# A decoder layer on one core: first maxima in banks of four diagonal squares or of the squares below them, a third cross tile's scores copied out by ScalarE, and the steps in another order

## The chip, the cores and the metric

One NeuronCore of a Trainium2 chip runs the whole kernel. The metric is the device time of one execution in microseconds (us). TensorE (PE) multiplies matrices, VectorE (DVE), ScalarE (ACT) and GpSimd (POOL) do the elementwise work, and SyncE (SP) issues most DMAs. The kernel is written in an explicit form: each engine runs its own list of instructions in order, and semaphores are the only tie between the lists.

## The reference

```python
x = layernorm(x + self_attention(x))          # 4 x 512 tokens of 256, 16 heads of 16, causal
x = layernorm(x + cross_attention(x, ctx))    # 16 heads of 64, 64 context rows of 192 per batch
x = layernorm(x + experts(x))                 # 8 experts, 256 -> 1024 -> 256, top 2, exact gelu
```

The self attention is a softmax over scores / 4 with everything above the diagonal masked; q, k and v have biases. The cross attention is a softmax over 64 context rows. The expert part routes each token to the two experts with the largest logits, weighs their outputs with a softmax over the two, and adds them. All is float32 in and out; the kernel multiplies in float16 pairs of a high and a low part (the function `three` issues three matmuls for one product).

## The kernel before

The program has two blocks. `attention_block` computes both attentions of all four batches and ends with the logits of most tokens; `expert_block` routes, gathers tokens by indirect DMA, runs 23 tiles of one or two blocks of 128 slots through their experts, scatters, adds and normalizes. The change touches only the first block.

Inside `attention_block` all work is cut into steps written `kind:batch:index`, and one long text, `ORDER`, lists them. Every engine goes through the whole list in that order and runs its own part of each step, so `ORDER` fixes the order within each engine. PSUM is shared by two rings: three banks M (kinds `xT, mT, ct, cx, o, xa, O, rt, lg, m, S, T`) and two double banks R (kinds `s, q, v, cT, W, kv, A, VW, idle`). `Slots` gives the steps of a ring their banks in the order of `ORDER`; PE waits until the previous user of a bank has been read out. PV is one more bank for the weighted sums.

The steps of a batch, in the order in which they depend on one another:

- `xT`, `q`, `v`: transpose the tokens, project. `ql` (POOL) makes the low parts, `store` and `stack` (SP) write q and k to DRAM and read them back as stacks of 48 rows per head pair (`qs`, `ks`), 12 DMAs.
- `m` (22 steps, index into `MAXES`): first pass over the scores, only for the row maxima. A step fills two M banks, one for the even and one for the odd heads, adds the causal mask by a matmul with `causal` (L227), and DVE reduces each bank (L237) into `rowmax`. `va` (POOL) adds the bias to v.
- `mT`, `max`: transpose the maxima (L964), negate (ACT, L646), write them as one more row of `qs` by two small DMAs.
- `s` (20 steps): the scores again, shifted by the maxima (PE L974), exponential (ACT L655), mask on the diagonal squares (POOL L526). `w` (12): weighted sums into PV (L988), `pv` (ACT L659) copies them, `ct`, `ct.n` transpose and divide.
- `cx`, `o`, `o.d`, `r`, `n`: transpose, output projection, residual, layernorm (`r` is the root on POOL, `n` the scaling on DVE).
- `x1b`, `xa`: add the bias (POOL), transpose. `S` (8 steps, two for each of four token tiles): cross scores. They leave PSUM in one of two ways. `S.d` (DVE): maximum over each head (L800), then the difference is written to `e_x` (L801). Or, for the last tile only, `S.c` (ACT, L668) copies both halves, `S.m` (DVE, L808) takes the maxima from SBUF, and `S.p` (POOL, L556) subtracts them. Then `xe` (exponential, ACT), `xs` (sum, DVE), `xp` (division, POOL L561), `T`, `T.l` (transposes, L1030), `O`, `O.d` (weighted sum and projection in one, 24 matmuls, L210), `r`, `n` into `x2_all`.
- `rt`, `lg`: router transposes and logits for 12 of the 16 token tiles.

The steps `cT, wk, W, kv, wo, A, VW` with `A.s`, `VW.s` (SP) fold the cross attention's weights with the context once for all batches and store the result in DRAM; `ax` and `vw` load the part of a batch. `idle:k:n` issues n matmuls of 512 columns on PE whose result nobody reads (L885); there are 129 of them: 43 ahead of the first `m`, 42 in fourteen groups of three between the `m` steps of batch 0, 16 each ahead of the `m` steps of batches 2 and 3, and 12 in the last batch's tail.

The work is interleaved across batches. While batch b's self attention runs (`s`, `w`), the `m` steps of batch b+1 run, and batch b-1's cross attention. Only batch 0's `m` steps and batch 3's cross attention stand nearly alone.

## Time and profile before

| | us |
|---|---|
| median of 3 runs | 726.97 |
| lowest, highest | 723.96, 730.16 |
| the profiled execution, whole | 724.8 |
| its span from the first to the last instruction | 723.1 |
| busy in the span: PE, DVE | 609.1, 534.3 |
| busy in the span: ACT, POOL | 393.3, 327.5 |

An engine is busy in the profile when an instruction that does work is on it. Matmuls are pipelined, so PE's busy time is an upper bound of what it needs. Weight loads (PEld) run beside the matmuls. The granted TensorE clock is given as a share of full speed. The idle time ahead of a group is followed by the engine and line that ended it.

### The profile page before, as it was taken

Reading aid. Unit: us, or ns where it says so; the run is one execution under the profiler, and the core shown is the slowest. Engines: PE = TensorE matmul, PEld = TensorE weight load, DVE = VectorE, ACT = ScalarE, POOL = GpSimd, SP = SyncE. Lnnn points to the kernel's source line nnn. Section 1 sums busy time; section 2 is a strip of 40 time slices with the busy share of each in tenths; the row PEclk is TensorE's granted clock in tenths of the full one; section 3 lists DMA queues with packets and bytes.
Section 4 is the critical chain, followed back from the end, with each engine's and each line's share of the span. In section 5 each row is a group of like instructions: output and inputs, shape, how many; then the busy total and the mean of one; then the engine's idle time right before and its main releaser. Section 6 shows DMA issues by size and latency. Waiting matters only on the chain. (4 is left out here: it accounts for less than half of the span.)

```text
span 723.1 us, 13495 instructions
## 1 busy us (share of the span) xinstructions
PE 609.1 (84%) x5180; PEld 412.0 (57%) x5180; DVE 534.3 (74%) x972; ACT 393.3 (54%) x587; POOL 327.5 (45%) x360
## 2 busy tenths in 40 slices
PE   7797778988899999888997761699999999999950
PEld 3452234443354635544564450589999999998840
DVE  4437856635877678876847848889999999999574
ACT  3543148784346434345551311367877877876534
POOL 9531024466146325425453321443755755761335
PEclk9899979999999999999999995589999999999965
DMA  8742715459001640111003003677788789785173
GB/s 234 211 57 87 117 60 175 146 180 230 2 1 38 102 154 1 59 30 61 1 2 117 1 0 125 242 270 244 276 271 303 260 272 305 247 291 196 56 247 116
DMA packets 74383, 104.66 MB, mean 145 GB/s; under 512 B 5184, under 2 KB 62216, under 8 KB 73296
## 3 DMA queue, kind: packets, MB, share of 16 engines
q1 hardware_dynamic: 70576, 93.58, 42.2%
q0 software_dynamic: 3744, 10.23, 4.3%
q8 instruction: 41, 0.67, 0.4%
q14 instruction: 22, 0.18, 0.1%
HBM read 81.84 MB, written 21.89 MB: 143 GB/s over the span
## 5 line engine op out<-in xcount | busy, mean ns | idle before, releaser
L237 DVE TENSOR_REDUCE rowmax<-M 128x1 f32<-128x384 f32 (+3 forms) x176 | 104.7, 636 | 45.4 <-PE M L227 43.6
L210 PE MATMUL HB<-xT,w 128*128 128x256 f16 (+1 forms) x1104 | 107.3, 257 | 0.0
L655 ACT ACTIVATE probs<-R 128x1024 f32<-128x1024 f32 x80 | 80.6, 1027 | 48.5 <-PE R L974 48.3
L1704 PE MATMUL YB<-w,h 128*128 128x256 f16 x936 | 105.9, 273 | 0.1
L210 PEld LDWEIGHTS HB<-xT,w 128*128 128x128 f16 x1104 | 94.9, 98 | 9.9 <-DVE xT L1557 0.6
L1704 PEld LDWEIGHTS YB<-w,h 128*128 128x128 f16 x936 | 91.5, 98 | 10.7 <-issue 0.4
L1400 ACT ACTIVATE hf<-HB,b 128x256 f32<-128x256 f32 (+1 forms) x184 | 70.4, 444 | 44.9 <-PE HB L210 41.4
L526 POOL TENSOR_SCALAR_AFFINE_SELECT probs<-probs 128x256 f32<-128x256 f32 x128 | 49.8, 411 | 92.7 <-ACT probs L655 92.2
L1296 POOL DMA_INDIRECT xg<-scratch_xs,src x39 | 77.2, 1980 | 26.2 <-issue 11.0
L1304 POOL DMA_INDIRECT scratch_ys<-y,dst x39 | 43.5, 1117 | 81.7 <-ACT y L1380 76.3
L1569 DVE SCALAR_TENSOR_TENSOR w<-w2f,w 128x2048 f16<-128x2048 f32 x23 | 52.6, 2285 | 9.2 <-ACT w L1386 8.2
L1584 DVE SCALAR_TENSOR_TENSOR h<-hf,h 128x512 f16<-128x512 f32 (+1 forms) x92 | 56.3, 612 | 3.2
L210 PE MATMUL M<-vw,pT 128*128 128x256 f16 x384 | 47.9, 285 | 6.6 <-DVE pT L694 6.3
L1562 DVE SCALAR_TENSOR_TENSOR w<-w1f,w 128x2048 f16<-128x2048 f32 x23 | 52.5, 2284 | 0.0
L1371 ACT ACTIVATE w<-w1f 128x2048 f16<-128x2048 f32 x23 | 44.3, 1925 | 14.4 <-DMA w1f<-in_W 14.4
L222 PE MATMUL M<-ks,qs 48*128 48x128 f16 (+3 forms) x256 | 34.2, 305 | 19.9 <-DVE rowmax L237 16.4
L210 PE MATMUL M<-a_x,x1T 128*128 128x512 f16 x192 | 45.4, 380 | 4.7 <-DVE x1T L694 2.2
L885 PE MATMUL R<-ident 128*128 128x512 f16 x129 | 36.8, 429 | 12.7 <-DVE v_diag L738 3.7
L561 POOL TENSOR_TENSOR e_x<-e_x,xinv 128x1024 f32<-128x1024 f32 x16 | 30.5, 1904 | 36.8 <-DVE xinv L814 36.8
L210 PEld LDWEIGHTS M<-vw,pT 128*128 128x128 f16 x384 | 38.3, 102 | 15.5 <-DVE pT L694 4.7
L1386 ACT ACTIVATE w<-w2f 128x2048 f16<-128x2048 f32 x23 | 44.3, 1927 | 1.4 <-DMA w2f<-in_W 1.4
L988 PE MATMUL PV<-probs,v_aug 128*32 128x256 f32 (+3 forms) x512 | 43.8, 441 | 1.4 <-POOL probs L526 1.4
(244 smaller groups left out, 1040.8 us busy)
## 6 DMA issues: line engine op xcount, KB each, us to landing
w1f<-in_W SPq DMA_DIRECT2D x23, 1024.0 KB
w2f<-in_W SPq DMA_DIRECT2D x23, 1024.0 KB
scratch_qk<-qk SPq DMA_DIRECT2D x8, 512.0 KB, 4.0
scratch_ax<-stage SPq DMA_DIRECT2D x16, 256.0 KB, 2.8
scratch_vw<-stage SPq DMA_DIRECT2D x16, 256.0 KB, 2.9
vw<-scratch_vw SPq DMA_DIRECT2D x4, 1024.0 KB, 6.1
a_x<-scratch_ax SPq DMA_DIRECT2D x4, 1024.0 KB, 7.6
parts<-scratch_ys SPq DMA_DIRECT2D x8, 512.0 KB, 7.7
```

What stands on the lines that cost most here:

```text
L210: last = nc.tensor.matmul(out, left(a, k), right(b, k), start=(k == 0 and m == 0), stop=(k == n - 1 and m == 2))
L237: return nc.vector.tensor_reduce(rowmax[:, t, par * PAIRS + p0:par * PAIRS + p0 + pairs], bank[:, 0:pairs * wide].rearrange("p (n w) -> p ...
L526: last = P.affine_select(out=diag, in_=diag, compare_op=ALU.is_ge, fill=0.0, base=0, pattern=[[0, 2], [1, 128]], channel_multiplier=-1)
L655: A.activation(probs[:, n % RING, :, :], bank[:, :, :], ACT.Exp, scale=1.0 / (QS * QS)).then_inc(empty, 1)
L1296: pool.indirect_dma_start(out=xg[:, n % 2, t, :], out_offset=None, in_=dram["xs"], in_offset=bass.IndirectOffsetOnAxis(src[:, at:at + 1], ...
L1371: A.activation(w1[:, q, 0, :, :].rearrange("p c f -> p (c f)"), w1f[:, q, :, :].rearrange("p c f -> p (c f)"), ACT.Copy, scale=WS).then_in ...
L1386: A.activation(w2[:, q, 0, :, :].rearrange("p m d -> p (m d)"), w2f[:, q, :, :].rearrange("p m d -> p (m d)"), ACT.Copy, scale=WS).then_in ...
L1400: last = A.activation(hf[:, 2 * b + m, 0:width(n)], HB[b][:, m, 0:width(n)], ACT.Gelu, bias=b1[:, 2 * b + m, WORK[n]:WORK[n] + 1], scale=1 ...
L1562: V.scalar_tensor_tensor(w1[:, q, 1, :, :].rearrange("p c f -> p (c f)"), w1f[:, q, :, :].rearrange("p c f -> p (c f)"), WS, w1[:, q, 0, : ...
L1569: V.scalar_tensor_tensor(w2[:, q, 1, :, :].rearrange("p m d -> p (m d)"), w2f[:, q, :, :].rearrange("p m d -> p (m d)"), WS, w2[:, q, 0, : ...
L1584: V.scalar_tensor_tensor(h[:, q, 1, pair, at], hf[:, pair, at], XS, h[:, q, 0, pair, at], ALU.mult, ALU.subtract).then_inc(h_split, 1)
L1704: last = M.matmul(YB[q][:, t, :], h[:, q, a, m, t * 128:t * 128 + 128], w2[:, q, b, m, :], start=((m, a, b) == (0, 0, 0)), stop=((m, a) == ...
```

## The change

1. `MAXES` is cut otherwise. Before, a step took the whole row of squares of a token tile, 1 to 4 squares wide, for as many head pairs as fit, and its mask covered only the diagonal squares. Now a step is either "diagonal" (the four diagonal squares of two tiles and two head pairs, 8 matmuls of 128 columns and one mask matmul of 512 columns for each bank) or "below" (the squares below the diagonal of one tile, no mask). There are still 22 steps a batch: 8 diagonal ones, 2 below of tile 1, 4 below of tile 2 (all 512 columns), and 8 below of tile 3 (384 columns). The maxima below the diagonal go to a buffer of their own, and a new step `mc` (DVE) combines the two; `mT` waits for it.
2. For batches 0 to 2 the third tile's cross scores (`S` index 4 and 5) also leave by `S.c`, `S.m`, `S.p`, `xe`; for batch 3 nothing changes.
3. `ORDER` is replaced. Its marks: the idle matmuls ahead of and within batch 0's `m` steps, and those ahead of `m:2:0` and `m:3:0`, are gone, and 35 stand in the tail of batch 3; `q:1:1`, `v:1:0`, `kv:3:0` and `A:0:0` stand between the first `m` steps, `wo.l` ahead of them and `kv.l:3:0` behind them; `w:0:9` to `w:0:11` and `pv:0:3` stand ahead of `mT:1:0`; `stack:2:0` stands ahead of the stores of the last fold pieces.
4. Buffers are laid out so that `ctxT` and `x1` no longer lie where the folded weights are made; the wait for all fold pieces moves from `cx` and `x1b` to the loads `ax` and `vw`, the one for `wout` from the first `s` to the first `xa` and `x1b`.
5. The rest of the diff is bookkeeping for a batch split in halves, and `SPLIT = (0, 0, 0, 0)` keeps every batch whole: the `s`, `w`, `pv`, `ct` work and its widths are as before.

```diff
 def max_items():
     items = []
-    for t in range(NQ):
-        pairs = max(1, 512 // (128 * (t + 1)))
-        if PAIRS % pairs:
-            pairs = 1
-        items += [(t, p, pairs) for p in range(0, PAIRS, pairs)]
+    for t in (0, 2):
+        items += [("diagonal", t, p, 2) for p in range(0, PAIRS, 2)]
+        for u in (t, t + 1):
+            pairs = 512 // (128 * u) if u in (1, 2) else 1
+            items += [("below", u, p, pairs) for p in range(0, PAIRS, pairs) if u > 0]
     return items
+COPIED = ((2, 3), (2, 3), (2, 3), (3,))
+SPLIT = (0, 0, 0, 0)
...
 ORDER = """
+xT:0:0 wh:0:0 xT.l:0:0 xT:0:1 xT.l:0:1 wh:0:1 q:0:0 x_in:1:0 cT:0:0 cT.l:0:0 wk:0:0 wh:1:0 wk.l:0:0 wh:1:1 wk:1:0
+ql:0:0 q:0:1 ql:0:1 v:0:0 W:0:0 cT:1:0 wk.l:1:0 W.l:0:0 wk:2:0 xT:1:0 wo:0:0 wk.l:2:0 xT.l:1:0 xT:1:1 va:0:0 cT.l:1:0
+xT.l:1:1 W:1:0 store:0:0 kv:0:0 W.l:1:0 kv.l:0:0 stack:0:0 kv:1:0 wo.l:0:0 kv.l:1:0 q:1:0 kv:2:0 ql:1:0 m:0:0 kv.l:2:0
+m:0:1 q:1:1 m:0:2 m:0:3 v:1:0 m:0:4 ql:1:1 m:0:5 kv:3:0 m:0:6 m:0:7 m:0:8 A:0:0 m:0:9 m:0:10 m:0:11 m:0:12 m:0:13
+m:0:14 A.l:0:0 m:0:15 m:0:16 x_in:2:0 m:0:17 store:1:0 A.s:0:0 m:0:18 m:0:19 m:0:20 m:0:21 mc:0:0 stack:1:0 kv.l:3:0
+mT:0:0 max:0:0 m:1:0 VW:0:0 VW.l:0:0 VW.s:0:0 A:1:0 A.l:1:0 s:0:0 A.s:1:0 xT:2:0 s:0:1 wg:0:0 xT.l:2:0 VW:1:0 s:0:2
...
+VW.s:6:0 pv:0:3 ct.n:0:2 m:1:20 A:7:0 m:1:21 va:1:0 ct:0:3 mc:1:0 mT:1:0 ct.n:0:3 max:1:0 cx:0:0 cx.l:0:0 cx:0:1 v:2:0
+A.l:7:0 stack:2:0 A.s:7:0 cx.l:0:1 s:1:0 o:0:0 o.d:0:0 o:0:1 s:1:1 r:0:0 o.d:0:1 xT:3:0 s:1:2 VW:7:0 r:0:1 xT.l:3:0
+VW.l:7:0 n:0:0 m:2:0 n:0:1 VW.s:7:0 s:1:3 w:1:0 m:2:1 x1b:0:0 m:2:2 xa:0:0 xa.l:0:0 m:2:3 xa:0:1 xa.l:0:1 m:2:4 s:1:4
...
+S:3:2 S.d:3:2 xp:3:0 lg:5:0 lg.l:5:0 S:3:3 S.d:3:3 T:3:0 T.l:3:0 T:3:1 T.l:3:1 xe:3:1 S:3:4 xs:3:1 O:3:0 S.d:3:4 S:3:5 xp:3:1
+O.d:3:0 S.d:3:5 T:3:2 T.l:3:2 T:3:3 T.l:3:3 S:3:6 xe:3:2 S.c:3:6 S:3:7 xs:3:2 xp:3:2 S.c:3:7 S.m:3:3 O:3:1 O.d:3:1
+T:3:4 S.p:3:3 T.l:3:4 T:3:5 xe:3:3 r:3:2 T.l:3:5 O:3:2 xs:3:3 n:3:2 O.d:3:2 xp:3:3 T:3:6 T.l:3:6 T:3:7 T.l:3:7 O:3:3
...
 def score_maxima(nc, k, banks, n, qs, ks):
+    kind, t, p0, pairs = MAXES[n]
+    if kind == "below":
+        wide = 128 * t
+        for p in range(pairs):
+            for par in range(2):
+                rows = slice(64 * par, 64 * par + STACK)
+                last = nc.tensor.matmul(banks[par][:, p * wide:p * wide + wide],
+                                           qs[rows, p0 + p, t * 128:t * 128 + 128], ks[rows, p0 + p, 0:wide],
+                                           start=p == 0, stop=p == pairs - 1)
...
+    for i in range(2):
+        for p in range(pairs):
+            for par in range(2):
+                rows, at = slice(64 * par, 64 * par + STACK), (i * pairs + p) * 128
+                cols = slice((t + i) * 128, (t + i) * 128 + 128)
+                nc.tensor.matmul(banks[par][:, at:at + 128], qs[rows, p0 + p, cols], ks[rows, p0 + p, cols],
+                                 start=(i, p) == (0, 0), stop=False)
     for par in range(2):
+        yield nc.tensor.matmul(banks[par][:, :].rearrange("p (n w) -> p n w", w=128), k["ident16"][:, :],
+                               k["causal"][:, :].unsqueeze(1).to_broadcast([128, 4, 128]), start=False, stop=True)
...
+def reduce_maxima(nc, rowmax, below, bank, n, par):
+    kind, t, p0, pairs = MAXES[n]
+    heads = slice(par * PAIRS + p0, par * PAIRS + p0 + pairs)
+    if kind == "below":
+        return nc.vector.tensor_reduce(below[:, t, heads], bank[:, 0:pairs * 128 * t].rearrange("p (n w) -> p n w", n=pairs),
+                                       AX.X, ALU.max)
+    return nc.vector.tensor_reduce(rowmax[:, t:t + 2, heads],
+                                   bank[:, :].rearrange("p (t n w) -> p t n w", t=2, n=pairs), AX.X, ALU.max)
...
+            elif kind == "mc":
+                rows = half_rows(b, n)
+                first = max(rows.start, 1)
+                for m in maxima_of(b, n)[-2:]:
+                    for side in SIDES:
+                        freed_slot(dve, g, side, b, m)
+                V.tensor_tensor(rowmax[:, first:rows.stop, :], rowmax[:, first:rows.stop, :],
+                                below[:, first:rows.stop, :], ALU.max).then_inc(max_done, 1)
...
             elif kind == "mT":
+                pe.wait_ge(max_done, combined.upto("mc", b, n))
...
             elif kind == "xe":
-                if n == NQ - 1:
-                    act.wait_ge(x_shifted, b + 1)
+                if n in COPIED[b]:
+                    act.wait_ge(x_shifted, shifted.upto("S.p", b, n))
...
             elif kind == "vw":
-                if b > 0:
+                if b == 0:
+                    fold_done(sp)
+                else:
                     filled(sp, g, "O", b - 1, NQ - 1)
```

## Rows read from the trace of the kernel before

**Rows 1.** Stretches: length, busy PE, PEld, DVE, ACT, POOL (instructions), PEclk, DMA share, GB/s.

```profile
46.00:94.00 48.00, 36.70 (x241) 15.09 (x240) 34.15 (x50) 10.37 (x12) 6.98 (x6) 0.90 0.38 77
94.00:156.00 62.00, 54.39 (x507) 28.63 (x505) 38.31 (x58) 47.04 (x69) 29.32 (x37) 0.97 0.43 138
156.00:240.00 84.00, 74.96 (x612) 37.66 (x612) 59.86 (x111) 43.00 (x58) 40.08 (x57) 1.00 0.31 82
240.00:320.00 80.00, 72.19 (x589) 38.75 (x588) 63.28 (x123) 34.30 (x44) 32.07 (x49) 0.98 0.28 67
320.00:381.00 61.00, 54.91 (x501) 31.92 (x499) 39.01 (x84) 34.30 (x45) 31.27 (x51) 1.00 0.10 32
381.00:435.00 54.00, 37.23 (x267) 25.46 (x268) 35.94 (x73) 11.71 (x18) 16.30 (x18) 0.97 0.08 35
435.00:723.00 288.00, 241.09 (x2279) 214.12 (x2277) 246.28 (x457) 190.46 (x313) 141.55 (x122) 0.88 0.69 234
```

**Rows 2.** The chain that ended last, where it leaves the attention part.

```profile
434.73 0.64 PE XB L1659 x4
```

**Rows 3.** DVE's groups by shape from 46 to 94 us.

```profile
L237 DVE TENSOR_REDUCE rowmax<-M 128x1 f32<-128x512 f32 x16 | 10.3, 686 | 4.2 <-PE M L227 3.6
L237 DVE TENSOR_REDUCE rowmax<-M 128x1 f32<-128x384 f32 x16 | 8.2, 553 | 3.0 <-PE M L227 2.9
L237 DVE TENSOR_REDUCE rowmax<-M 128x2 f32<-128x512 f32 x8 | 5.1, 684 | 2.0 <-PE M L227 2.0
L738 DVE SCALAR_TENSOR_TENSOR v_diag<-R,v_diag 64x1024 f16<-64x1024 f32 x4 | 4.9, 1217 | 0.0
L237 DVE TENSOR_REDUCE rowmax<-M 128x4 f32<-128x512 f32 x4 | 2.6, 685 | 6.5 <-PE M L227 6.5
```

**Rows 4.** Instructions in order of time from the start to batch 0's first `m` step.

```profile
19.78 2.13 POOL L505 TENSOR_TENSOR qk<-qf,qk 128x1024 f16<-128x1024 f32 x1
...
43.65 2.78 PE L210 MATMUL R<-w_hl,xT 128*128 128x256 f16 x24
...
46.37 0.40 PE L222 MATMUL M<-ks,qs 48*128 48x128 f16 x8
...
47.12 1.29 DVE L237 TENSOR_REDUCE rowmax<-M 128x4 f32<-128x512 f32 x2 [3.69 <-PE M L227]
```

**Rows 5.** The same view within batch 0's `m` steps and at batch 1's first.

```profile
69.47 1.02 DVE L237 TENSOR_REDUCE rowmax<-M 128x1 f32<-128x384 f32 x2 [0.22 <-PE M L227]
...
93.57 1.01 PE L964 MATMUL M<-ident,rowmax 128*16 128x128 f32 x4 [1.48 <-DVE rowmax L237]
...
94.52 0.61 PE L222 MATMUL M<-ks,qs 48*128 48x128 f16 x8
...
95.70 1.29 DVE L237 TENSOR_REDUCE rowmax<-M 128x4 f32<-128x512 f32 x2 [2.39 <-PE M L227]
```

**Rows 6.** SP and DVE in order of time, up to batch 2's first `m` step.

```profile
160.89 3.86 SPq L435 DMA_DIRECT2D qs<-scratch_qk  x6
...
175.94 1.29 DVE L237 TENSOR_REDUCE rowmax<-M 128x4 f32<-128x512 f32 x2 [4.04 <-PE M L227]
```

**Rows 7.** The page's or the groups' rows for the cross scores' ways out of PSUM.

```profile
L801 DVE TENSOR_TENSOR e_x<-M,xmax 128x512 f32<-128x512 f32 x24 | 16.6, 691 | 0.8
L800 DVE TENSOR_REDUCE xmax<-M 128x8 f32<-128x512 f32 x24 | 16.1, 670 | 4.2 <-PE M L210 4.1
L556 POOL TENSOR_TENSOR e_x<-e_x,xmax 128x1024 f32<-128x1024 f32 x4 | 7.6, 1902 | 0.1
L808 DVE TENSOR_REDUCE xmax<-e_x 128x16 f32<-128x1024 f32 x4 | 4.9, 1214 | 0.3 <-ACT e_x L668 0.3
L668 ACT ACTIVATE e_x<-M 128x512 f32<-128x512 f32 x8 | 4.8, 599 | 5.7 <-PE M L210 5.7
```

**Rows 8.** PE in order of time in the tail of batch 3.

```profile
415.52 4.45 PE L210 MATMUL M<-vw,pT 128*128 128x256 f16 x24 [2.22 <-DVE pT L694]
...
422.89 2.78 PE L210 MATMUL M<-vw,pT 128*128 128x256 f16 x24 [2.04 <-DVE pT L694]
```

More of the change, by code:

```diff
@@ new lines, with use_of_item, reader_of, last_sum @@
+WORK_SUMS = [sums_of(b) for b in range(NB)]
+def use_of_item(b, n):
+    return sum(len(ITEMS[before]) for before in range(b)) + n
+READERS = {use_of_item(b, i): (b, n) for b in range(NB) for n, (_, _, terms) in enumerate(WORK_SUMS[b])
+           for _, _, i, _ in terms}
+def reader_of(use):
+    return READERS[use]
+def last_sum(b, u):
+    return max(n for n, (unit, _, _) in enumerate(WORK_SUMS[b]) if unit == u)
+def item_width(b, n):
+    u, item = ITEMS[b][n]
+    _, first, end = UNITS[b][u]
+    return max(at + 128 * (end - max(j, first)) for _, j, at in item)
@@ L89, with halves_upto @@
+def halves_upto(b, part):
+    return sum(parts(k) > part for k in range(b + 1))
+EARLY = NT // 2 - 2 + SPLIT[NB - 1]
 PIECES = [(kind, n) for n in range(2 * NB) for kind in ("A", "VW")]
@@ L187, with __init__ @@
 class Tally:
-    def __init__(self, *kinds):
-        self.place = {step: n + 1 for n, step in enumerate(step for step in STEPS if step[0] in kinds)}
+    def __init__(self, *kinds, only=None):
+        steps = [step for step in STEPS if step[0] in kinds and (only is None or only(*step))]
+        self.place = {step: n + 1 for n, step in enumerate(steps)}
     def upto(self, *step):
@@ L644, in _ @@
                 bank, empty = filled(act, g, kind, b, n)
-                positive(act, max_in, 32 * b)
-                A.activation(neg_maxT[:, :], bank[0:H, :], ACT.Copy, scale=-1.0).then_inc(empty, 1)
+                for before in range(b):
+                    for part in range(parts(before)):
+                        act.wait_ge(max_in[part], 32 * halves_upto(before, part))
+                cols = half_cols(b, n)
+                A.activation(neg_maxT[:, cols], bank[0:H, cols], ACT.Copy, scale=-1.0).then_inc(empty, 1)
             elif kind == "s":
@@ L972, in _ @@
                     for par in range(2):
                         rows = slice(64 * par, 64 * par + ROWS)
[L974 to L975 removed]
+                        last = M.matmul(bank[:, par, at:at + 128 * end - q], ks[b % 2][rows, p, 128 * j:128 * j + 128],
+                                        qs[b % 2][rows, p, q:128 * end], start=True, stop=True)
```

342 lines of the change are left out of this document (184 added, 158 removed), and 4 rows, old and new, of the table SUMS.

## The prediction

> **What bounds the kernel now.** I read the stretches first [rows 1]; from 94 us on they are cut where a batch's `mT` runs, then where batch 3's self attention ends. Next comes the chain that ended last [rows 2]. From 434.7 us on the chain runs through the router, the experts and the final layernorm without a break. The change issues nothing there, so the 288.4 us from 434.7 to the end of the span stay as they are, and the question is when the attention part ends. It has three kinds of stretch. From 46 to 94 us, with batch 0's first maxima, no engine is full: DVE is busy 34.2 of 48.0 us, PE 36.7, and some 9 of PE's are idle matmuls: 24 matmuls of 256 columns take 2.78 us [rows 4], so one of 512 about 0.22, and there are 42. From 94 to 381 us three batches overlap; PE is busy 54.4 + 75.0 + 72.2 + 54.9 = 256.5 of 287 us and nothing else is above 80% in any row. The reader should see there that PE's queue, in order, is the bound, with 30.5 us of gaps and 32 idle matmuls, 7 us. From 381 to 435 us batch 3's cross attention stands alone, PE is busy 37.2 of 54 us and DVE 35.9: a chain of short dependent steps.
>
> **The work of the first maxima** is neither more nor less. Per batch DVE reduces 14 steps of 2 x 512 and 8 of 2 x 384 columns before and after; by [rows 3] that is 28 x 0.685 + 16 x 0.553 = 28.0 us of instruction time both times. That a reduction now gives four maxima of 128 instead of one of 512 costs nothing: forms with 1, 2 and 4 outputs take 686, 684 and 685 ns. On PE a step with 8 matmuls of 128 columns and two masks of 512 takes 0.77 us from its start to the next step's (46.37 to 47.14 in [rows 4]: 0.40 for the first part, 0.60 for the masks, overlapping); the steps below the diagonal lose their masks and become shorter. PE's columns are equal, 64 + 48 score matmuls and 16 masks replace 64 and 44, so there are 20 more weight loads a batch and 28 fewer short masks. I take 0, with bounds of -1 and +2 us in the PE-bound stretches for four batches. `mc` adds a DVE operation of 48 elements, some 0.2 us, estimated from the reductions (0.685 and 0.553 us for 512 and 384 columns [rows 3] leave 0.16 fixed and 0.001 a column), and a wait of PE's `mT` for it. Behind that wait PE has `m:b+1:0` and `s`; before, `mT` waited for the same reductions, so four times 0.2 us is all.
>
> **Term A, the stretch of batch 0's maxima.** The first step started at 46.37 us, right behind `v:1` [rows 4], and `mT:0` at 93.57 us [rows 5]. Its start hardly moves: the chain to it is `ql:0:0` on POOL at 19.78 us [rows 4], which stands behind POOL's memsets and is untouched, then `store`, `stack` and their DMAs. PE no longer has `q:1:1` and `v:1` ahead of it, so it starts when the stack has landed, 0 to 1.5 us earlier. From there DVE was busy 34.2 us and idle 13.9 [rows 1]: waits for PE of 3.6 + 2.9 + 2.0 + 6.5 us stood ahead of the reductions [rows 3]. After the change DVE has 28.0 us of reductions, 2.43 us of `kv.l:2` (two of 1.217 [rows 3]) and `mc`; `wo.l`, the key pieces and `kv.l:3` have left. What idles it now: `q:1:1`, `v:1` and `kv:3` on PE, each 2.6 to 2.8 us as `v:1` was in [rows 4], against 1.3 us of reductions of the step before, so 1.3 to 2 us each, together 5; and the diagonal steps, whose first bank is full 0.75 us after the start (46.37 to 47.12) against the 0.65 us that DVE has left on the step before, 8 x 0.1 us. The 0.22 us ahead of each 384-column step [rows 5] go, as no mask stands behind them. 28.0 + 2.6 + 5 + 0.8 makes 36.4 us where there were 47.2, 10.8 less. Against it: the 42 idle matmuls are gone. Where the clock is low, a diagonal step takes 1.18 us to its first full bank (94.52 to 95.70 in [rows 5]) instead of 0.75. If the second half of the stretch is at that clock, this is 4 x 0.43 us, and `kv.l:3` (2.43 us), now between `mc` and the reductions of `m:1:0`, holds `VW:0` about 1 us. I take 10.8 - 1.7 - 1.1 = 8 us gained, bounds 0 and 12.
>
> **Term B, the stack of batch 2.** Its DMAs were issued from 160.89 us, some 5 us behind `mT:1` at 156 us, because the small maxima DMAs and the stores of the last fold pieces stood ahead of them; DVE then waited 4.0 us for the first `m` step at 175.94 us, while PE filled the time with idle matmuls [rows 6]. In the new order the stack stands ahead of those stores, 2 to 3 us earlier. The stores are what is queued behind it, 12 issues of 0.64 us; their reader `ax:0` is 8 us later for that in SP's order, and `S:0:0` comes late enough not to see most of it. 2 us gained, bounds -2 and 4. Batch 3's stack is issued behind `max:2:0` in both orders.
>
> **Term C, the copied cross scores.** In batches 0, 1 and 2 each takes two reductions and two subtractions from DVE, 2 x (0.670 + 0.691) = 2.72 us, and adds one reduction of 1.21; ACT gets 2 x 0.60 and POOL 1.90 us [rows 7]. DVE is relieved of 1.5 us a batch in stretches where it isn't the bound. The M bank is free after 0.6 instead of 1.36 us, which helps PE, but the exponential comes later: 0.60 + 1.21 + 1.90 = 3.7 us behind the last score matmul instead of 1.36, and POOL's masks of `probs` queue behind the 1.90 us. I take 0, with 3 x 1.4 = 4 us better (all of the relief counts) and 3 x 2.35 = 7 us worse (all of the latency counts) as the bounds.
>
> **Term D, the tail.** `O:3:1` started at 415.52 us, 2.2 us late for `pT`, and took 4.45 us at a low clock, where `O:3:2` took 2.78 [rows 8]. Now `T:3:2` and `T:3:3` stand ahead of `S:3:6`, so `pT` is ready when the scores are done; 35 idle matmuls stand earlier in the tail. The late start (2.2) and the clock (1.7) are worth up to 3.9 us; the last tile's chain through POOL then limits. 3 us gained, bounds 0 and 5.
>
> **Term E, the rest of the order** between 94 and 381 us. PE's sum is unchanged but for the 7 us of idle matmuls, which stood in waits for the stacks and give nothing by themselves; three weighted sums move ahead of `mT:1`, which shifts work between stretches only. `va:1` moves behind batch 1's maxima on POOL; who waits is ACT's `v:2`, also moved back. The 30.5 us of gaps are what an order can win or lose. The profile can't say which; I take 0, bounds -8 and +8.
>
> Sum: 8 + 2 + 0 + 3 + 0 = 13 us, less four times 0.2 for `mc`: 12. The profiled execution of before took 724.8 us, 1.7 more than its span; so 713 on its scale. The median of the three runs stands 2.2 us higher, in a spread of 6.2; I say 713.
>
> **The clock, by rows and by a page.** In the rows the clock is below full in every stretch with gaps on PE: 0.90 from 46 to 94 us even with the idle matmuls, 0.97 in the tail [rows 1]. The Trainium skill (TensorE: Matmul & The Clock Gate, A second HAM failure mode: psum-queue depth-cycling) tells of a kernel that cycles through PSUM banks, where PE's short idles between groups let the clock fall again and again. That is the shape of batch 0's maxima without their idle matmuls, and by that rule the second rival below would be the outcome; the trace before cannot show it, as it never runs those steps bare.
>
> **The rivals.** (1) The gain of term A is given back: an earlier `mT:0` only moves batch 1's work into a PE queue that is 90% busy, and the later waits grow by as much. For it speaks the 256.5 of 287 us; against it that the work of 94 to 381 us depends on `mT:0` for its start and nothing else there has a fixed time. It leaves B and D: 725 - 5 + 2 = 722. (2) Slower: the clock stays at 1.2 GHz from the start to 94 us. Then `q:1:1`, `v:1`, `kv:3` take twice 2.6 and DVE idles 7.8 us more; 8 diagonal steps lose 0.43 us each, 3.4; the fourteen others 0.1 each; and `kv:0`, `kv:1`, `q:1:0`, `kv:2` ahead of `m:0:0` double, which starts it 7 us later than before. 10.8 - 7.8 - 3.4 - 1.4 - 7 is 9 us lost; with B and D 729, and 734 without them. It decides against the change from about half of that stretch at the low clock on, and PE's long run of dense matmuls right ahead of `m:0:0` speaks against it. (3) The latency of term C is on the path in all three batches: 7 us, so 720. (4) The order closes a third of the gaps between 94 and 381 us and the relief of DVE counts: 713 - 10 = 703.
>
> **How the numbers follow.** A measurement of this kernel tells about 1%, 7 us, from no change. Forecast, 713: 0.45. Rival 4, 703: 0.15. Rival 1, 722: 0.16. Rival 3, 720: 0.10. Rival 2, 729 to 734: 0.14. Faster by over 1% (below 719.7) are the forecast, rival 4 and half of rival 3: 0.65. Within 1%: rival 1, the other half of 3 and a little of 2: 0.22. Slower: 0.13. The range goes from 701, under rival 4, to 731, into rival 2.
>
> **What the profile after would show.** Term A: `mT:0` (L964) at 84 to 87 us instead of 93.6, waits for PE ahead of the reductions of that stretch near 6 us instead of 15, the clock there not below 0.7. B: batch 2's first reduction 16 us or less behind `mT:1` (20 before), its wait gone or under 2 us. C: L801 18 times, L668 14 times, and no wait of `xe` for POOL over 3 us. D: `O:3:1` in one piece of 2.8 us and 50 to 51 us from the end of batch 3's self attention to the router, 54 before. E: PE's gaps between `mT:0` and that end near 30 us. The prediction is wrong if the clock falls in batch 0's maxima, or if those gaps move by more than 8 us.

## The result and the profile after

The changed kernel takes 742.7 us, the median of four runs (741.2 to 744.4), where the kernel before takes 727.1 (724.0 to 730.2): a ratio of 1.020, 95% interval 1.016 to 1.024. It is slower, by 15.7 us, and outside the predicted range. The profiled executions have spans of 742.6 and 723.1 us; the one of after was the slowest of its four and the one of before nearly the fastest, so the stretches below add up to 19.5 us and not to 15.7.

First the stretches of the kernel after, cut at the same events as [rows 1]: batch 0's first `m` steps, the four `mT`, the end of batch 3's self attention, the router. Columns as there.

```profile
46.50:90.00 43.50, 29.16 (x231) 13.41 (x229) 28.66 (x47) 12.00 (x17) 6.36 (x3) 0.81 0.38 71
90.00:159.00 69.00, 55.92 (x540) 28.31 (x540) 39.55 (x63) 48.21 (x70) 34.07 (x45) 0.93 0.42 132
159.00:245.00 86.00, 67.87 (x564) 33.76 (x564) 56.57 (x104) 42.02 (x57) 38.08 (x52) 0.94 0.32 87
245.00:337.60 92.60, 75.15 (x624) 41.53 (x624) 66.07 (x123) 36.99 (x47) 36.39 (x54) 0.93 0.21 47
337.60:398.00 60.40, 55.60 (x504) 32.63 (x504) 39.79 (x80) 34.33 (x46) 31.32 (x48) 1.00 0.14 45
398.00:452.30 54.30, 40.30 (x287) 26.57 (x287) 38.33 (x77) 12.14 (x19) 17.04 (x17) 0.99 0.06 20
452.30:742.60 290.30, 242.22 (x2279) 215.06 (x2279) 246.72 (x457) 190.48 (x313) 139.44 (x123) 0.88 0.69 232
```

Two things stand out beside [rows 1]. The clock is under 0.95 in every row from 46 to 337 us, where it was 0.97 to 1.00 from `mT:0` on. And PE's gaps have grown: from `mT:0` to the end of batch 3's self attention it is busy 55.9 + 67.9 + 75.2 + 55.6 = 254.5 of 308 us, where it was 256.5 of 287. Without the 32 idle matmuls (7 us) PE was busy 249.6 us before: it now takes 5 us more for the same useful work, at a lower clock, and waits 53 us instead of 30.

The same events in all kernels of this study, by the start of each `mT` matmul (L964 before, L1100 after), of the last `pv` copy and of the router's first transposes. This is where each kernel gains or loses; one profile each, and a stretch whose steps are the same differs by up to 3 us between kernels (`mT:0` to `mT:1` takes 69.3, 67.7 and 66.4 us in after, e3 and e5):

| kernel | to mT:0 | mT:0 to 1 | mT:1 to 2 | mT:2 to 3 | to end of batch 3's sums | tail | span |
|---|---|---|---|---|---|---|---|
| before | 93.6 | 61.2 | 84.8 | 79.3 | 61.4 | 54.5 | 723.1 |
| after | 90.2 | 69.3 | 85.8 | 92.4 | 60.1 | 54.6 | 742.6 |
| e1 new maxima in the old order | 93.3 | 65.0 | 86.4 | 78.8 | 61.4 | 56.1 | 728.7 |
| e2 copies in the old order | 93.8 | 61.4 | 91.6 | 83.2 | 63.7 | 56.1 | 737.7 |
| e3 after + idle matmuls at the stacks | 89.7 | 67.7 | 84.6 | 89.2 | 61.7 | 56.1 | 737.5 |
| e4 e3 + idle matmuls up to mT:0 | 82.4 | 68.8 | 87.6 | 90.3 | 60.1 | 55.5 | 733.4 |
| e5 after, first m of 2 and 3 later | 90.4 | 66.4 | 86.4 | 85.4 | 60.1 | 54.6 | 733.5 |
| e6 after without copies | 90.4 | 69.1 | 87.9 | 94.8 | 60.6 | 55.5 | 748.4 |
| e7 e6 without new maxima | 92.5 | 67.5 | 90.7 | 96.8 | 61.3 | 55.4 | 752.3 |
| e8 before without idle matmuls | 95.0 | 63.7 | 87.6 | 79.6 | 61.4 | 58.1 | 733.2 |
| e9 e5 + idle matmuls up to mT:0 | 81.9 | 69.6 | 84.3 | 85.5 | 61.5 | 54.6 | 727.3 |
| e10 new order to mT:0, the rest old | 83.8 | 60.8 | 84.8 | 77.6 | 61.5 | 54.6 | 711.5 |
| e11 e10 with new maxima | 82.4 | 66.0 | 86.5 | 78.8 | 61.4 | 54.6 | 718.5 |
| e12 e4 + idle matmuls late | 81.9 | 69.3 | 87.3 | 89.2 | 61.3 | 54.6 | 732.6 |
| e13 e11 without idle matmuls in front | 89.4 | 63.5 | 86.3 | 79.2 | 61.4 | 56.3 | 725.2 |
| e14 new order to mT:1 | 82.3 | 72.0 | 86.2 | 79.5 | 61.3 | 56.1 | 726.1 |
| e15 new order to mT:2 | 92.7 | 70.5 | 90.6 | 77.7 | 61.4 | 56.2 | 740.2 |
| e16 new order to mT:3 | 92.4 | 69.2 | 87.0 | 93.4 | 62.6 | 54.4 | 749.1 |

After against before: 3.4 us gained to `mT:0`, 8.1 lost to `mT:1`, 1.0 to `mT:2`, 13.1 to `mT:3`, 1.3 gained, 0.1 and, in the expert part, 1.9 lost. Sum 19.5.

**Batch 0's maxima.** The groups of DVE from 46.5 to 90.2 us, answering [rows 3]:

```profile
L330 DVE TENSOR_REDUCE rowmax<-M 128x4 f32<-128x512 f32 x16 | 10.3, 686 | 10.9 <-PE M L319 10.9
L328 DVE TENSOR_REDUCE below_max<-M 128x1 f32<-128x384 f32 x16 | 8.2, 553 | 1.4 <-PE M L305 1.4
L328 DVE TENSOR_REDUCE below_max<-M 128x2 f32<-128x512 f32 x8 | 5.1, 686 | 0.3 <-PE M L305 0.3
L859 DVE SCALAR_TENSOR_TENSOR v_diag<-R,v_diag 64x1024 f16<-64x1024 f32 x3 | 3.7, 1218 | 0.3 <-ACT v_diag L733 0.2
L328 DVE TENSOR_REDUCE below_max<-M 128x4 f32<-128x512 f32 x4 | 2.5, 685 | 1.9 <-PE M L305 1.9
L891 DVE TENSOR_TENSOR rowmax<-rowmax,below_max 128x48 f32<-128x48 f32 x1 | 0.2, 209 | 0.1
```

The reductions cost what [rows 3] said, 28 us, and the waits for PE went from 15 us to 14.5, of which 6.6 stand ahead of the very first reduction. PE in order of time shows why:

```profile
42.50 0.82 PE L1054 MATMUL R<-cT,wkv 128*128 128x256 f16 x3
43.26 0.82 PE L1056 MATMUL R<-cT,wkv 64*128 64x256 f16 x3
44.01 5.05 PE L292 MATMUL R<-xT,w_hl 128*128 128x512 f16 x12
48.90 0.49 PE L1054 MATMUL R<-cT,wkv 128*128 128x256 f16 x3
...
51.92 0.28 PE L316 MATMUL M<-ks,qs 48*128 48x128 f16 x2
...
87.00 0.50 PE L305 MATMUL M<-ks,qs 48*128 48x384 f16 x2 [0.72 <-DVE below_max L328]
88.22 0.51 PE L305 MATMUL M<-ks,qs 48*128 48x384 f16 x2 [0.71 <-DVE below_max L328]
90.15 1.02 PE L1100 MATMUL M<-ident,rowmax 128*16 128x128 f32 x4 [1.43 <-DVE rowmax L891]
```

Up to 48 us three matmuls of `kv` take 0.82 us, behind it 0.49; `q:1:0` takes 5.05 us where such a projection takes 2.75 at full clock (batch 0's first, at 9.96 us in e4). So the first `m` step starts at 51.92 us and not at 46.37 [rows 4]: 5.5 us lost ahead of the stretch. The stretch itself went from 47.2 to 38.2 us. The clock by windows, 32 to 48 and 76 to 92 us (PEclk is the last column but two):

```profile
32.00:48.00 16.00, 16.00 (x58) 5.93 (x59) 6.49 (x5) 2.85 (x3) 0.07 (x1) 0.50 0.74 132
76.00:92.00 16.00, 6.27 (x28) 1.77 (x28) 14.08 (x25) 0.59 (x1) 1.09 (x1) 0.50 0.89 133
```

0.50 is the lower of the two clock levels, 1.2 GHz. In the first window PE is busy all the time, with waits of 1.29 and 1.20 us before it, and runs the whole of `kv:0` and `kv:1` low; in the second it alternates 0.50 us of work with 0.71 us of waiting and costs little, since DVE, busy 14.1 of 16 us, sets the pace there. The Trainium skill (TensorE: Matmul & The Clock Gate, A second HAM failure mode: psum-queue depth-cycling) says that short idles between groups of matmuls let the clock fall; by that rule, the 76 to 92 us window agrees.

**The stacks of batches 2 and 3.** PE's queue at `m:2:0`, at `m:3:0` and behind it:

```profile
175.22 0.61 PE L316 MATMUL M<-ks,qs 48*128 48x128 f16 x8 [5.70 <-DMA ks<-scratch_qk]
...
254.86 0.39 PE L1112 MATMUL R<-qs,ks 64*128 64x512 f16 x2
255.18 1.48 PE L292 MATMUL M<-w_hl,ctxT 128*128 128x256 f16 x12
261.88 0.61 PE L316 MATMUL M<-ks,qs 48*128 48x128 f16 x8 [5.21 <-DMA ks<-scratch_qk]
262.42 1.03 PE L319 MATMUL M<-causal,ident 128*128 128x512 f16 x2
263.25 4.68 PE L292 MATMUL R<-w_hl,xT 128*128 128x256 f16 x24
```

PE stands 5.70 and 5.21 us with nothing to do until `ks` lands, and what follows runs at the low clock: `v:3` takes 4.68 us where `v:1` took 2.78 [rows 4]. And all that stands behind `m:3:0` in the queue, `v:3`, scores and an output projection, needed no stack. Batch 2's stack was not issued late on SP:

```profile
162.16 3.83 SPq L545 DMA_DIRECT2D qs<-scratch_qk  x6
166.03 3.81 SPq L545 DMA_DIRECT2D ks<-scratch_qk  x6
```

Its DMAs start 2.7 us behind `mT:1` (159.44), before 6.1 (160.89 in [rows 6] against 154.79). The stack is earlier, as term B had it, but `m:2:0` stands 15.8 us behind `mT:1` instead of 20.4, with only 10 us of other work ahead of it.

**The copied tiles.** Groups answering [rows 7], over the whole kernel:

```profile
L673 POOL TENSOR_TENSOR e_x<-e_x,xmax 128x1024 f32<-128x1024 f32 x7 | 13.3, 1901 | 1.1 <-DVE xmax L937 1.1
L930 DVE TENSOR_TENSOR e_x<-M,xmax 128x512 f32<-128x512 f32 x18 | 12.4, 691 | 0.6
L789 ACT ACTIVATE e_x<-M 128x512 f32<-128x512 f32 x14 | 8.5, 604 | 8.2 <-PE M L292 8.2
```

The counts are those foretold, 18 and 14, each operation costs what it did, and no exponential (L796) waits for POOL's subtraction, where before 5.1 us of such waits stood in two places.

**The tail.** `O:3:1` and the last two:

```profile
433.85 2.78 PE L292 MATMUL M<-vw,pT 128*128 128x256 f16 x24
436.47 1.04 PE L1175 MATMUL M<-ident,e_x 128*128 128x128 f32 x8
439.62 2.78 PE L292 MATMUL M<-vw,pT 128*128 128x256 f16 x24 [2.11 <-DVE pT L815]
...
445.69 2.78 PE L292 MATMUL M<-vw,pT 128*128 128x256 f16 x24 [1.62 <-DVE pT L815]
```

The router's first transposes (L1803) start at 452.34 us, in [rows 2] at 434.73. `O:3:1` has no wait and takes 2.78 us, so the 2.2 and 1.7 us of [rows 8] are gone. The tail is no shorter all the same. `S:3:6` now stands behind `T:3:2` and `T:3:3`, and DVE's maxima of the copied last tile (`S.m`) start 37.0 us behind the end of the self attention (434.76 against 397.74), before 33.4 (413.61 against 380.25). Of these 3.6 us 1.7 are there before any cross score: `S:3:0` starts at 413.76, 16.0 us behind that end, before at 394.58, 14.3 behind. DVE copies router transposes for 1.4 us (from 405.35) ahead of the second residual, and the second group of 14 idle matmuls keeps PE until 411.1, when its next input had been ready since 410.5. What `O:3:1` gained, the last tile's scores lost.

### The profile page after: what moved, and what is told of

Same layout as the page of the kernel before. It is cut to its first block and busy times, and to the rows that moved or that the text cites. A ratio compares the mean times of both kernels' runs of the same rounds, so it can differ in the third digit from the quotient of the medians.

```text
span 742.6 us, 13593 instructions
## 1 busy us (share of the span) xinstructions
PE 598.3 (81%) x5166; PEld 406.8 (55%) x5166; DVE 538.0 (72%) x967; ACT 396.3 (53%) x593; POOL 330.8 (45%) x363
## 5 line engine op out<-in xcount | busy, mean ns | idle before, releaser
L1440 POOL DMA_INDIRECT xg<-scratch_xs,src x39 | 74.8, 1917 | 26.4 <-issue 11.0
L328 DVE TENSOR_REDUCE below_max<-M 128x1 f32<-128x384 f32 (+2 forms) x112 | 63.2, 608 | 22.9 <-PE M L305 22.3
L330 DVE TENSOR_REDUCE rowmax<-M 128x4 f32<-128x512 f32 x64 | 41.1, 684 | 32.6 <-PE M L319 32.5
L1131 PE MATMUL PV<-probs,v_aug 128*32 128x256 f32 (+3 forms) x512 | 45.4, 452 | 3.0 <-POOL probs L641 2.8
L678 POOL TENSOR_TENSOR e_x<-e_x,xinv 128x1024 f32<-128x1024 f32 x16 | 30.5, 1904 | 32.2 <-DVE xinv L943 32.1
L305 PE MATMUL M<-ks,qs 48*128 48x128 f16 (+2 forms) x192 | 22.5, 296 | 22.4 <-DVE below_max L328 18.1
```

Source lines behind the costliest of these rows:

```text
L328: return nc.vector.tensor_reduce(below[:, t, heads], bank[:, 0:pairs * 128 * t].rearrange("p (n w) -> p n w", n=pairs), AX.X, ALU.max)
L1131: last = M.matmul(PV[32 * hd:32 * hd + 32, q:128 * end], v_aug[:, b % 2, j, 4 * gr + hd, :], probs[:, use_of_item(b, i) % RING, par, at:at ...
L1440: pool.indirect_dma_start(out=xg[:, n % 2, t, :], out_offset=None, in_=dram["xs"], in_offset=bass.IndirectOffsetOnAxis(src[:, at:at + 1], ...
```

## The experiments

Each ratio is to runs of the kernel before taken beside it on the same chip. After was not run beside the experiments, so a comparison with it is given by the medians and by the ratios (1.020 is 14.5 us); where the two differ much, the size is uncertain by as much.

**One part alone, in the order of before.** e1 has the new `MAXES`, the new reductions and `mc:b:0` ahead of each `mT:b:0`. e2 has only the copies:

```diff
-S.d:b:4 ... S.d:b:5            (b = 0, 1, 2)
+S.c:b:4 ... S.c:b:5 ... S.m:b:2 S.p:b:2 xe:b:2
```

> The kernel before, in its own order with all its idle matmuls, with only the first maxima cut in the new way and mc directly ahead of each mT. Theory P (the loss comes from the order: TensorE reaches the m step that waits for a stack with no other work ahead of it, stands idle there, and runs on at the low clock): no difference that can be told, 724 to 730 us. Rival M (the new cut itself costs, because a diagonal step holds TensorE 0.77 us with its 512-column masks and DVE waits for it): 732 us or more, and DVE's waits ahead of the reductions grow by 5 us or more.

> The kernel before with only the third cross tile's scores of batches 0 to 2 copied out by ScalarE, S.m and S.p directly ahead of xe. Theory P: within 3 us of the kernel before, 724 to 730 us. Rival C (the longer way through S.c, S.m and S.p, 3.7 instead of 1.36 us to the exponential, ends up on the path in three batches): 732 to 734 us, with waits of xe for POOL of 2 us and more.

e1: 730.4 us, 1.0035 (1.0013 to 1.0056). e2: 739.5 us, 1.015 (1.010 to 1.020). The new maxima cost 2.5 us by the ratio and 3.9 by the medians; the stretch from `mT:0` to `mT:1` is 3.8 us longer. The copies cost 11 us by the ratio and 13 by the medians, more than the bound of 7. That is also more than was expected of the longer way (732 to 734 us). In e2 ACT's exponential and POOL's subtraction meet in ACT's order, which the groups show:

```profile
L677 ACT ACTIVATE e_x<-e_x 128x1024 f32<-128x1024 f32 x16 | 16.9, 1059 | 33.5 <-DVE e_x L803 18.5 <-POOL e_x L558 14.9
L223 PE MATMUL M<-ks,qs 48*128 48x384 f16 x64 | 11.7, 356 | 14.7 <-DVE rowmax L238 5.8 <-ACT e_x L670 5.0 <-DVE pT L696 2.8
```

ACT waits 14.9 us for POOL, where it waited 5.1 in the kernel before, and PE's `m` steps wait 5.0 us for banks M that ACT has yet to copy out. That place in the order, `S.m` and `S.p` directly ahead of `xe`, was mine.

**The same parts taken out of the new order.** e6 is after with the third tile by `S.d`; e7 is e6 with the old maxima and no `mc`, so that the order and the layout are all that differs from before.

> The changed kernel with the third cross tile's scores of batches 0 to 2 read out by DVE again (S.d in the places of S.c, S.m:b:2 and S.p:b:2 gone). In the order of before the copies cost 11 us. If their cost is a matter of the longer way itself, the changed kernel gets back a like amount, 731 to 735 us. If it is a matter of where the steps stand in ScalarE's queue, and the new order, made for the copies, places them well, it stays at 740 to 744 us.

> The changed kernel with the third tile read by DVE and the first maxima cut as before, mc gone: only the order and the layout of the buffers differ from before. The new cut in the order of before cost 2.5 us. If the parts add up, this is 2 to 3 us under e6_third_by_dve; what is left over the 726.5 us of before is the price of the order alone, which theory P puts at 5 us or more.

e6: 749.1 us, 1.032 (1.027 to 1.037). e7: 754.7 us, 1.039 (1.034 to 1.044). Neither came as expected: e6 was to be 731 to 735 or 740 to 744 us, e7 faster than e6. In the new order the copies gain 6.3 us by the medians (749.1 to 742.7) and 9 by the ratios, and the maxima 5.6 (754.7 to 749.1); the intervals of e6 and e7 overlap. The order by itself, with its layout of buffers, loses 28 us. So the loss is the order's, and the two other parts, bad in the old order, pay some of it back in the new.

**Idle matmuls given back.** e3 puts 20 ahead of `m:2:0` and of `m:3:0`. e4 also has 43 ahead of batch 0's first `m` and three ahead of each of `m:0:8` to `m:0:21`, into bank PV since R is in use:

```diff
+idle:4:20 m:2:0   ...   idle:5:20 m:3:0                                    (e3 and e4)
+warm:0:7 xT:0:0   warm:1:14 q:0:0   warm:2:8 q:0:1   warm:3:14 kv:0:0      (e4)
+warm:8:3 m:0:8    ...   warm:21:3 m:0:21                                   (e4)
```

> The changed kernel with 20 idle matmuls ahead of m:2:0 and 20 ahead of m:3:0, where TensorE waited 5.7 and 5.2 us for the stack, and nothing else. Theory P in the form that the clock is the price: both waits are still there in time, but what follows runs at the full clock (v:3 took 4.68 us against 2.78, the maxima steps and sums behind the waits alike), 2 to 3 us back for each, so 736 to 739 us. Theory P in the form that the missing overlap is the price, and not the clock: 741 to 743 us.

> The kernel e3_idle_at_stack_waits with idle matmuls also where the kernel before had them in batch 0: 43 ahead of the first m step and three ahead of each of its last fourteen steps, written to the sums' bank, which nobody uses by then. If the clock of the first 90 us matters (0.83 and 0.79 in the changed kernel, 0.93 and 0.90 before), mT:0 comes 3 us or more earlier than its 90.2 us and the whole gains 3 us over e3; if not, it is the same as e3 within 1 us, or slower by what the idle matmuls take from TensorE.

e3: 738.3 us, 1.0125 (1.008 to 1.017). e4: 735.1 us, 1.010 (1.007 to 1.014). With both, 7.6 of the 15.7 us come back. The step from e3 to e4 is 3.2 us by the medians and 1.5 by the ratios, though `mT:0` comes 7.3 us earlier: here a part of the earlier `mT:0` is given back. The stretches that answer to the low windows above, in e4:

```profile
32.00:48.00 16.00, 15.34 (x110) 7.38 (x108) 7.13 (x7) 6.50 (x8) 2.12 (x1) 1.00 0.87 132
46.00:82.40 36.40, 31.19 (x234) 13.47 (x232) 28.65 (x48) 9.15 (x13) 5.14 (x3) 1.00 0.44 84
```

The clock is 1.00, the first `m` step starts at 45.05 us, and `mT:0` at 82.41, 11.2 us earlier than before. The stretch takes 37.4 us; the prediction had 36.4.

**Idle matmuls taken from before.** e8 is before without its 129.

> The kernel before with all 129 idle matmuls taken out and nothing else changed. If they are the whole difference in clock (0.934 against 0.905 of the changed kernel) and the clock is the price, 733 to 738 us, with low-clock stretches behind both stacks and in batch 0's maxima; if they only fill slack, 725 to 729 us.

735.0 us, 1.012 (1.007 to 1.017). In the old order they are worth 8.7 us by the ratio and 9.7 by the medians, though nobody reads what they compute. The span is 10.1 us longer, and it is spread: 1.4, 2.5, 2.8, 0.3, 0 and 3.6 us by the table.

**The first `m` step of batches 2 and 3 later.** e5 moves `m:2:0` to just ahead of `m:2:1` and `m:3:0` to just ahead of `m:3:1`; nothing is added. e9 does the same with e4's matmuls up to `mT:0` and none at the stacks.

```diff
-m:3:0 v:3:0 s:2:2 o:1:1 o.d:1:1 s:2:3 w:2:0 m:3:1
+v:3:0 s:2:2 o:1:1 o.d:1:1 s:2:3 w:2:0 m:3:0 m:3:1
```

> The changed kernel with m:2:0 and m:3:0 each moved to directly ahead of m:2:1 and m:3:1, so that s:1:3 and w:1:0, and v:3, s:2:2, o:1:1, s:2:3 and w:2:0, stand ahead of the wait for the stack in TensorE's queue instead of behind it. Theory P (the missing overlap is the larger price): batch 3's wait of 5.2 us shrinks to 1 us or less, batch 2's 5.7 us to about 3, and the low clock behind them goes, 6 to 9 us in all, 734 to 737 us. Theory Q (the waits are slack that the stretch gives back anyway, since DVE or the chain of the cross attention sets its end): 741 to 744 us.

> The changed kernel with m:2:0 and m:3:0 moved back as in e5_first_maxima_later and the idle matmuls of batch 0 as in e4_idle_everywhere, none at the stacks. The move brought 5 us and batch 0's idle matmuls about 3 us beyond those at the stacks, with mT:0 at 82 us. If the two add, 731 to 734 us. If the earlier mT:0 is used up by waits further on (rival 1 of the prediction), 736 to 738 us, with mT:0 at 82 and batch 3's mT as late as in e5.

e5: 737.6 us, 1.017 (1.013 to 1.021), less than after by 5.2 us by the medians and 2 by the ratios, with overlapping intervals. In its trace `m:3:0` waits for nothing, but `m:2:0` still waits 4.46 us for `ks`, for only `s:1:3` and `w:1:0` moved ahead of it; its stretch, `mT:1` to `mT:2`, is no shorter (86.4 us against 85.8). From `mT:2` to `mT:3` it takes 85.4 us where after took 92.4 and e3, which filled the same wait with idle matmuls, 89.2. In that stretch useful work in the wait gives 7.0 us and idle matmuls 3.2. Over the kernel e5 and e3 can't be told apart: 5.2 against 4.4 us by the medians, 2 against 5.4 by the ratios. e9 against e4 can, and both have the same front: e9 takes 729.3 us, 1.002 (0.999 to 1.005), 6 us less than e4, whose interval lies above. So the moved steps are worth more than idle matmuls in their place, and the two edits of e9 together undo 13.4 us of the change.

**More clock late.** e12 is e4 with three idle matmuls ahead of five `m` steps of batch 2 (16, 18 to 21) and six of batch 3 (9 to 14), where e4's clock was still low.

> e4_idle_everywhere with three more idle matmuls ahead of m:2:16, 18, 19, 20, 21 and of m:3:9 to m:3:14, where its granted clock fell (224 to 240 and 308 to 318 us). If the low clock there is the price, 3 us or more back, 729 to 732 us. If the stretches are DVE's (reductions in a row while TensorE has little to do), 734 to 737 us, with the clock at full speed there.

735.6 us, 1.009 (1.006 to 1.012), as e4. Batch 3's stretch in e12:

```profile
238.40:327.70 89.30, 78.92 (x663) 42.65 (x664) 65.02 (x123) 36.99 (x47) 36.33 (x53) 1.00 0.22 48
```

and in e4:

```profile
238.80:329.00 90.20, 78.17 (x644) 43.57 (x644) 65.91 (x122) 37.08 (x48) 36.33 (x53) 0.93 0.22 48
```

The clock goes from 0.93 to 1.00 and the stretch loses 0.9 us, less than such stretches differ by from kernel to kernel. There the clock was a sign of waiting, not its price. From `mT:0` to the end of batch 3's sums e12 takes 307.1 us with a clock of 0.98, where e11 below, at the same 0.98 and in the old order, takes 292.7.

**New order only up to `mT:0`.** e10 has the old maxima, no copies, the new order as far as `mT:0` with e4's matmuls, and from there the order of before. e11 is e10 with the new maxima and `mc`.

> The old cut of the maxima and DVE for the third tile; the new order up to mT:0 with the idle matmuls of batch 0, and from there on the order of before. Term A of the prediction by itself. If an earlier mT:0 carries through (as the prediction had it), 716 to 719 us, mT:0 at 83 to 85 us and every later mark 8 to 10 us earlier than before. If it is given back in TensorE's full queue (rival 1), 724 to 727 us.

> e10_new_front_old_rest with the new cut of the maxima and mc. The new cut cost 2.5 us in the order of before and brought 5.6 us in the new order. If its worth depends on the order around it, batch 0's part is no slower here (mT:0 within 1 us of e10 or earlier) and the whole is 1 to 4 us slower than e10. If it is better by itself, the whole is 2 us or more faster.

e10: 716.9 us, 0.985 (0.980 to 0.991). e11: 720.7 us, 0.990 (0.986 to 0.994). e10 beats both kernels by more than its interval; its profile is of its fastest execution (713.2 us, the others 716.3 to 723.3). Its stretches:

```profile
46.50:83.80 37.30, 31.32 (x212) 13.82 (x212) 28.35 (x47) 8.64 (x13) 7.26 (x7) 1.00 0.43 85
83.80:144.60 60.80, 53.44 (x500) 28.84 (x501) 39.01 (x60) 46.13 (x67) 28.01 (x37) 0.97 0.43 134
```

`mT:0` is 9.7 us earlier, and every later stretch keeps its length within 0.2 us or shortens. The new maxima cost e11 3.8 us against e10, in the traces most of it between `mT:0` and `mT:1` (66.0 against 60.8 us), though the two intervals overlap.

**Where the rest of the loss sits.** e13 is e11 without the idle matmuls in front. e14, e15 and e16 have the new maxima, no copies and e4's matmuls in front, and take the new order up to `mT:1`, `mT:2` and `mT:3`, the old one from there. At each stack stand the idle matmuls of the order that it lies in: 16 in the old one, e4's 20 in the new one.

> New steps up to mT:0 and new maxima, then the steps of before, as in the kernel that took 720.7 us, but without the 43 matmuls ahead of the first m step and the 42 between batch 0's m steps. If the clock is what those matmuls bought: mT:0 at 90 us instead of 82.4, the clock at half speed for some of 32 to 48 and 76 to 92 us, and 727 to 731 us, no better than before. If the new steps of the front are what gained and the idle matmuls are incidental: 719 to 723 us.

> The new order as far as mT:1 with the idle matmuls in batch 0, then the steps of before; new maxima, the third tile by DVE. Beside the version that changes at mT:0 (720.7 us). If the middle of the new order costs where its stretches are long: 66.0 us from mT:0 to mT:1 become 69, the rest keeps its lengths, 722 to 726 us. If the three weighted sums drawn ahead of mT:1 are work only moved: the longer stretch is given back in the next one and the time is 719 to 722 us.

> The new order as far as mT:2, with 20 idle matmuls ahead of m:2:0, then the steps of before. If the loss sits in the stretch from mT:2 to mT:3: 723 to 728 us, one or two more than with the change at mT:1. If it is spread over the whole middle: 728 to 732 us.

> The new order as far as mT:3, with 20 idle matmuls ahead of m:2:0 and m:3:0, then the steps of before. If the stretch from mT:2 to mT:3 holds the loss that the idle matmuls don't explain: it takes 88 to 91 us instead of 79, and the time is 733 to 738 us, 8 to 11 more than with the change at mT:2. If that stretch only takes over work from the next, the one behind mT:3 is shorter by as much and the time stays below 730 us.

Beside these four the kernel before took 723.8 to 746.7 us, so their ratios settle nothing (e14 1.011, 0.996 to 1.026; e15 1.009, 1.000 to 1.019; e16 1.029, 1.015 to 1.043), and only the lengths of stretches in the table are read. By the medians e14, e15 and e16 took 731.3, 734.3 and 747.7 us, all longer than either outcome that was expected. In the profiles of e15 and e16 the first projection starts 10 us later than in e4 (9.96 us), which has the same steps in front, and so does all that follows. The rows show where the time goes. e4 first, then e16:

```profile
5.67 3.51 POOL L607 MEMSET ks<- 128x4096 f16 x1
6.74 2.46 DVE L831 TENSOR_SCALAR qk_bias<-qk_bias 128x2 f32<-128x2 f32 x1 [6.74 <-DMA qk_bias<-in_bk]
```

```profile
6.87 12.82 DVE L831 TENSOR_SCALAR qk_bias<-qk_bias 128x2 f32<-128x2 f32 x1 [6.87 <-DMA qk_bias<-in_bk]
...
17.78 1.80 POOL L608 MEMSET v_aug<- 128x2048 f32 x1
```

A DVE operation on two columns ends at 9.20 us in e4, where POOL's second large memset ends at 9.18. In e16 it ends at 19.69, 0.1 us behind the last of POOL's six large memsets, and the low parts of the first projection's operands queue behind it. In all eighteen profiles it ends at one of these two times. That is the pattern of the last section, and not the order; what decides in which gap between memsets DVE gets through, no run shows. e15's seven times lie in two groups, 730.7 to 734.3 and 740.3 to 743.8 us, as far apart as these 10 us; that the start makes the difference is an estimate, for only one of them has a trace. e13's `mT:0` is at 89.4 us instead of 82.4 in e11, and 5.8 of these 7.0 us are lost ahead of the first `m` step (50.96 against 45.16 us). The clock from 32 to 48 us is 0.52 in e13 and 1.00 in e11. Its profiled execution took 726.9 us (the others 722.4 to 736.1): most of the gain is gone. New order between `mT:0` and `mT:1` costs 69.2 to 72.0 us against 66.0 in e11, and the next stretch of e14 takes 86.2 us against 86.5, so nothing is given back. The table bears this out: with the new maxima this stretch takes 66.4 to 72.0 us in the ten kernels with the new order there, and 63.5 to 66.0 in the three with the old. From `mT:2` to `mT:3` it is 93.4 us in e16, 77.7 to 79.5 in e14 and e15, and behind it 62.6 against 61.4.

## Why the prediction was wrong, point by point

**The step that failed is term E**, "7 us of idle matmuls, which stood in waits for the stacks and give nothing by themselves", with the order's worth taken as 0 and bounded at 8 either way. The order alone costs 28 us (e7). From `mT:0` to the end of batch 3's sums the changed kernel takes 307.6 us where the kernel before took 286.7, 21 us more, and PE's gaps went from 30.5 to 53 us, beyond the 8 either way. The idle matmuls did give something: 4.4 us at the two stacks (e3 against after, 5.4 by the ratios), and useful work in their place 6 us more than they do (e9 against e4), the largest part of it, 4.8 us, between `mT:2` and `mT:3`.

What remains shows between e9 and e11, which have the same front and the same maxima: 301.0 against 292.7 us for the same matmuls, 8.3 us (e9 has the copies, e11 has not). By stretch it is 3.6 us more, 2.1 less, 6.7 more and 0.1 more. The 6.7 us between `mT:2` and `mT:3` (85.5 against 78.8) are not waits: PE does nothing useful for 12.9 us there in e9 and for 12.6 in e11 (9.0 of gaps, 3.6 of idle matmuls). The new order has `O:0:2` and its transposes behind `mT:2`, so the stretch holds 625 useful matmuls instead of 584 and 123 DVE operations instead of 119, while the one before it holds 564 instead of 623 and is only 2.1 us shorter. The three weighted sums ahead of `mT:1` are a like case, and e14 shows that they were not "shifted between stretches only": with them the first stretch grows and the next does not shrink. The lower clock (0.95 in e9, 0.98 in e11) doesn't settle the 8.3 us, since e12 has 0.98 and is no shorter than e4. Why a stretch that loses work doesn't shrink by as much stays open: no engine is full there, and no experiment separated the waits.

**Term A** (8 us, bounds 0 and 12) was right as a mechanism and gave 3.4. The stretch came down to 38.2 us, 37.4 with the clock full, for the 36.4 worked out. Wrong was the sentence "Its start hardly moves": the 5.5 us that `kv:0`, `kv:1` and `q:1:0` lose at 1.2 GHz came ahead of the stretch. The sum counts the 42 idle matmuls within the stretch and nowhere the 43 ahead of it, whose removal was so put at nothing; e13 against e11 gives 5.8 us for them and 1.2 for the 42. Rival 2 had the late start (7 us), but joined to a low clock in the whole stretch. "PE's long run of dense matmuls right ahead of `m:0:0`" did not keep the clock up: PE paused 1.29 and 1.20 us ahead of it, and it ran low from 32 to 48 us. The 10.8 us without deductions are nearly what e4 shows: a stretch 9.8 us shorter (37.4 against 47.2) and a start 1.3 us earlier.

**Term B** (2 us): the stack is issued 3.4 us earlier relative to `mT:1`, which fits the 2 to 3 us foretold (the "some 5 us" of before were 6.1, as `mT:1` ran at 154.79 and not at 156 us). But the wait moved from DVE to PE's head of queue, because `m:2:0` was drawn even further ahead than its stack. The cost is not DVE's 4.0 us but 5.7 us of PE with a cold clock behind it. At batch 3, where the prediction saw no change, the same happened: `m:3:0` ahead of `v:3`.

**Term C** (0, bounds 4 better and 7 worse) fails on both sides, by the order around it: 6.3 us or more better in the new order, 11 to 13 worse in the old with `S.m` and `S.p` right ahead of `xe`. A cost taken from rows of single operations had no order in it. That the changed kernel came out as well as it did is in part luck of this kind: terms put at 0 gave some 12 us back.

**Term D** (3 us): the late start and the low clock of `O:3:1` are gone as predicted, 3.9 us, and the tail is 54.6 us. "The last tile's chain through POOL then limits" was named and not priced, and the later start of the cross scores (1.7 us) was not foreseen.

**`mc`** was put at 0.8 us in all. PE waits 3.9 us for it in all:

```profile
L1100 PE MATMUL M<-ident,rowmax 128*16 128x128 f32 x16 | 2.8, 308 | 3.9 <-DVE rowmax L891 3.9
```

Most of that is the wait for the last reduction, which `mT` had before (L964 waited 3.2 us for `rowmax` in all); one `mc` took 1.07 us, below. **The maxima** were taken as 0 with bounds -1 and +2: 2.5 to 3.9 us worse in the old order (3.8 with the new front, e11 against e10), 5.6 better in the new.

**The rivals.** Rival 1, that the gain of A is given back, is refuted by e10 for the old order: an earlier `mT:0` carries through in full. In the new one e9 keeps it too (8.5 us earlier than e5, 8.2 us faster), and e4 keeps less than half (against e3). Rival 4, a better order, has the wrong sign. Rival 3's mechanism is real (e2) and is not in this change. Rival 2, slower by the clock, is the nearest in sign and in place, but priced the clock in front alone; that the clock also falls at the stacks, and the order's own waits, were in no rival.

## What to carry to other kernels

Put the first instruction that waits for a DMA behind all work of its queue that doesn't need that DMA: an in-order queue makes everything behind it wait. With two such steps moved the kernel took 6 us less than with idle matmuls in the waits (e9 against e4), and the stretch that gained most was the one whose wait went away altogether. Idle matmuls that look like waste are part of the schedule where TensorE would otherwise pause: price their removal by what the next dense run would cost at half the clock, and price it ahead of the stretch, too. Test an order in halves: with the new one up to a mark and the old one from there, one run shows which part gains (to `mT:0` with its idle matmuls, 10 us) and which loses. Compare such runs up to a mark where both have done the same work: a single stretch can be longer because a step was moved into it.
